# Pre-norm attention and expert layer: the second norm's rows are turned by VectorE through a DRAM scratch, and three small steps change engine or place

## The chip, the cores and the metric

The kernel runs on one core of a Trainium2 chip. A core has five engines with a queue of instructions each: TensorE (PE in the profile, its weight loads PEld), VectorE (DVE), ScalarE (ACT), GpSimd (POOL) and SyncE (SP), which only issues DMAs here. An engine takes its instructions in the order in which they are written; between engines there are semaphores. The metric is the device time of one execution in microseconds.

## The reference, cut to what matters

```python
x = hidden                                   # (2, 2048, 1024) f32, 4096 rows
h = layernorm(x)
q, k, v = h @ wq.T + bq, h @ wk.T + bk, h @ wv.T + bv      # 32 heads of 32 each
scores = einsum('bshd,bstd->bsht', q, k) / sqrt(32)   # over the HEADS of one row
context = einsum('bsht,bstd->bshd', softmax(scores), v)
x = x + context
h = layernorm(x)
gate = h @ gate_w.T                          # 8 experts, the best two are kept
w_full = one_hot(top2(gate)) * softmax(...)
low = h @ lora_A.T                           # 8 x 16 columns
x = x + h @ base_w.T + base_b + 2 * sum_e(w_full_e * low_e @ lora_B_e.T)
```

Attention runs between the 32 heads of one and the same row, so no row needs another one.

## The kernel before, in words

The 4096 rows are worked in T = 32 steps of P = 128 rows. Every f32 matmul operand is split into a float16 high part (a cast) and a float16 low part (original less high part), and a product is made of the terms high times high, high times low and low times high. The weights k, q, v, base and "ag" (lora_A with the gate, 136 columns) are split once, in the first two steps; where a weight's low part is all zero its term is skipped, which it is here for k, q and v, so a projection half of 512 columns is 16 matmuls (`project`, L1284).

Each engine's program is `pipeline` (L375): `step(0)`, `step(1)`, a loop over steps 2 to 30, `step(31)`, and a tail. A step t holds the attention front of tile t and the back of tile t-1 (called p = t-1 in the helpers). TensorE's order in a step before: first half of k (L1536); `context(t-1)`, 96 small matmuls of probabilities with v (L1541); second half of k; first half of q; the small matmul that spreads row statistics; second half of q; `turn2(t-1)`, 8 transposes of the normalised rows of tile t-1 (L1555); both halves of v; `experts(t-1)`, 24 matmuls with ag (L1562); `attend(scored)`, 96 small matmuls for the scores (L1568); `dense_all(t-1)` (L1456): 39 matmuls with base, `turn_low` (one transpose of the gated low-rank activations), 9 more, and `dense_lora` (L1433), which waits for `lowt_ready` and closes the sum.

The heads are turned by VectorE between the products: k's rows (`turn_first`, L1093), q's (L1204), v's (L1216) and the probabilities' (L1246). After each, ScalarE casts the high part (L743, L754, L759, L781) and VectorE or GpSimd subtracts to the low part: k's on VectorE (`first_low`), q's and v's on GpSimd (`second_lo` L529, `v_low` L535), the probabilities' on VectorE (L1253). The turned parts of k go out by 8 DMAs (`spread_k`, L424) into `diag`, block by block, because `attend` multiplies with block-diagonal operands; the parts of v are put there by 16 copies (`spread_v`, L356; line L360 in the rows), 12 on ScalarE and 4 on VectorE. `context` waits for all 16 and for the probabilities' low part.

The second norm: `attention_end` (L1066) turns the context back, adds the residual and takes the statistics; `norm2` (L1083) writes the normalised rows to `xn`; TensorE turns them (`turn2`) into `attn_ps`; ScalarE casts the high part `x2_hi` (L649), VectorE subtracts the low part `x2_lo` (L1004); then come `experts` and `dense`. The first norm of the next tile goes another way: its input is loaded a second time by DMAs that already permute 32-row blocks (`load_quads`, L416, four DMAs of 128-byte pieces), so one VectorE transpose (`turn_quads`, L993) turns it, and ScalarE casts it (`x1_high`, L644).

The gate (`gate_top` L1019, `gate_exp` L682, `gate_rest` L1029) gives `low`, the low-rank activations times the gate's weights; `turn_low` turns it on TensorE, and ScalarE's `low_copy` (L687, instruction L690) brings it back to SBUF and raises `lowt_ready`, for which `dense_lora` waits.

`soft` is the buffer of the softmax: written at L1226, and read for the last time at L1246.

Of the kernel before, what the change touches and what calls it, by code (L numbers as in the profile page):

```python
# [27 lines left out]
P = 128  # L28
# [37 lines left out]
def block_kernel(nc, x, wT, agT, lora_b, biases, out):  # L66
    T = x.shape[0] // P
    with ExitStack() as ctx:
# [166 lines left out]
        w_loaded = {g: [sem(f"w_{g}_loaded{k}") for k in range(KC)] for g in GROUPS}  # L235
# [111 lines left out]

        block = ctx.enter_context(nc.Block())
# [3 lines left out]
        x1_last = soft  # L352

# [18 lines left out]
        def rows(ap, t):  # L372
            return ap[bass.ds(t * P, P), :]

# [11 lines left out]
        def _(sp):  # L386
# [108 lines left out]
        def _(pool):  # L495
# [66 lines left out]
            def step(t, prev, nxt):  # L562
# [7 lines left out]
                if prev:  # L570
                    second_lo(t)
# [9 lines left out]
        def _(act):  # L581
# [52 lines left out]
            def x1_high(t):  # L634
# [5 lines left out]
                else:  # L640

                    act.wait_ge(x1_turned_ready, t)
                    act.wait_ge(scored, t)
                    nc.scalar.copy(x_hi[:, :, :], x1_turned).then_inc(xhi_ready, 1)  # L644

            def x2_high(p):

                act.wait_ge(turned2, p + 1)
                nc.scalar.copy(x2_hi, rows_ps).then_inc(x2hi_ready, 1)  # L649
# [80 lines left out]
            def step(t, prev, nxt):  # L730
# [15 lines left out]
                x2_high(t - 1)  # L746
# [7 lines left out]
                nc.scalar.copy(dense_parts[:, :, 0, :], turned3).then_inc(b_hi_ready, 1)  # L754

# [26 lines left out]
                if nxt:  # L782
                    for c in C_ACT_LAST:
# [12 lines left out]
        def _(dve):  # L796
# [208 lines left out]

            selectors()
# [76 lines left out]
            def norm2(p, x1):  # L1083
# [4 lines left out]
                else:  # L1088

                    dve.wait_ge(turned2, p)  # L1090
# [86 lines left out]
            def step(t, prev, nxt):  # L1177
                if not prev:
                    return first_step()
                if prev:  # L1180
# [10 lines left out]
                    norm2(t - 1, x1)  # L1191
                    turn_first(t)
# [7 lines left out]
                x2_low(t - 1)  # L1200
# [6 lines left out]
                add_bias(t, 0, "v", 1, v_acc, v_biased)  # L1207
                if nxt:
                    turn_quads(t + 1)
# [8 lines left out]
                if prev:  # L1218
                    gate_top(t - 1)

                dve.wait_ge(scored, t + 1)
                scores = attn_ps[:, :].rearrange("p (t c) -> p t c", t=QD)
# [5 lines left out]
                if one:  # L1228
                    base_split(6, 7)
                if nxt:  # L1230
# [47 lines left out]
        def _(pe):  # L1278
# [5 lines left out]
            def project(g, n, bank, done):  # L1284
# [14 lines left out]
                for k in range(KC):  # L1299
                    mm = nc.tensor.matmul(dst, x_lo[:, k, :], w_hi[g][:, k, cols], start=False, stop=(k == KC - 1))  # L1300
# [6 lines left out]
            def gram(g, first, last):  # L1307

                n_last = GRAM_CHUNKS[g] - 1
                for k in range(first, last):  # L1310
# [6 lines left out]
                    else:  # L1317
                        pe.wait_ge(w_loaded[g][k], 16)
# [86 lines left out]
            def experts(p):  # L1405

                pe.wait_ge(x2hi_ready, p + 1)
                pe.wait_ge(x2lo_ready, p + 1)
# [3 lines left out]
                for k in range(KC):  # L1412
                    nc.tensor.matmul(dst, x2_hi[:, k, :], ag_hi[:, k, :], start=(k == 0), stop=False)  # L1413
                    nc.tensor.matmul(dst, x2_hi[:, k, :], ag_lo[:, k, :], start=False, stop=False)  # L1414
                    mm = nc.tensor.matmul(dst, x2_lo[:, k, :], ag_hi[:, k, :], start=False, stop=(k == KC - 1))  # L1415
                mm.then_inc(ag_acc, 1)

# [22 lines left out]

            def dense_halves(p):

                pe.wait_ge(base_free, 2 * p + 1)
                dense(0, 0, KC)
# [11 lines left out]
            def dense_all(p):  # L1456

                pe.wait_ge(base_free, 2 * p + 1)
                dense(0, 0, KC)
# [68 lines left out]
            def step(t, prev, nxt):  # L1528
# [7 lines left out]
                project(FIRST, 0, 0, a_acc)  # L1536
                one = isinstance(t, int) and t == 1
                if one:
                    spread_flag(1)
                else:  # L1540
                    context(t - 1)  # L1541
# [6 lines left out]
                pe.wait_ge(v_biased, 2 * t)  # L1548
                project(SECOND, 0, 2, b_acc)
                if nxt:  # L1550
                    spread_stats(t + 1)

                pe.wait_ge(a_biased, 2 * t + 1)
                project(SECOND, 1, 0, b_acc)
                turn2(t - 1)  # L1555
# [6 lines left out]
                experts(t - 1)  # L1562
# [5 lines left out]
                attend(scored)  # L1568

                if one:  # L1570
                    dense_first()
# [65 lines left out]
```

## Time and profile before

| what | us |
|---|---|
| median of 3 runs | 1314.05 (1313.95 to 1314.11) |
| the profiled execution: device time | 1315.04 |
| the profiled execution: span of the core | 1313.2 |
| TensorE busy | 1286.7 (98%) |
| VectorE busy | 1106.1 (84%) |
| ScalarE busy | 672.4 (51%) |
| GpSimd busy | 278.7 (21%) |

The profile is one execution, taken by the hardware profiler. Its time line counts from the core's first instruction. Busy time is not the same as need: a matmul's row says when it was in the array, and whether its engine waited is read from the gaps and from what ended them. The loop's steps repeat closely; the step taken here as the example begins at 592.61 us and ends at 631.06 us.

### The profile page before, as it was taken

To read this page: it belongs to the slowest core of one execution; us is meant where nothing else is said; L and a number is where in the kernel's file an instruction comes from. 1 tells how busy PE (TensorE), PEld (TensorE's weight loads), DVE (VectorE), ACT (ScalarE), POOL (GpSimd) and SP (SyncE) were. 2 spreads that over 40 slices of the span, in tenths; PEclk is the share of its full clock that TensorE was granted. 3 is DMA by queue.
4 is the path that set the end of the run, shared out by engine and by line. 5 is a ranking of instruction groups with operands and counts; after the bars stand their busy time and mean duration, and the time that the engine had idled before them with its cause. 6 is when DMAs were issued, how large, how long until landed. Compare 5 with 4: busy or idle time off the path is not lost.

```text
span 1313.2 us, 30329 instructions
## 1 busy us (share of the span) xinstructions
PE 1286.7 (98%) x12506; PEld 682.2 (52%) x12506; DVE 1106.1 (84%) x1576; ACT 672.4 (51%) x1029; POOL 278.7 (21%) x305
## 2 busy tenths in 40 slices
PE   6899999999999999999999999999999999999998
PEld 4554554555555455555555555555555555555554
DVE  5799888888988888888888888888888888888885
ACT  4865445555444555544555554455554445545431
POOL 0212211212221121222112122211222221222220
PEclk9899999999999999999999999999999999999999
DMA  9732332221233222233322223322212322221210
GB/s 361 265 82 65 82 80 64 64 64 60 67 80 80 62 66 58 55 78 80 80 58 70 55 57 80 80 71 65 72 50 62 80 80 64 68 74 49 48 50 33
DMA packets 162011, 103.72 MB, mean 79 GB/s; under 512 B 135616, under 2 KB 136640, under 8 KB 161984
## 3 DMA queue, kind: packets, MB, share of 16 engines
q1 hardware_dynamic: 161984, 103.36, 28.1%
q8 instruction: 17, 0.28, 0.1%
q14 instruction: 10, 0.08, 0.0%
HBM read 69.78 MB, written 16.78 MB: 66 GB/s over the span
## 4 chain that ended last, share of the span: by engine, by line
PE 88%; DVE 6%; DMA 2%; ACT 1%; issue 1%; SPq 0%; DVEq 0%; POOL 0%; ACTq 0%
PE acc L1291 24%; PE acc L1300 24%; PE dense_acc L1430 23%; PE attn_ps L1383 7%; PE dense_acc L1438 4%; PE attn_ps L1391 2%; DMA work<-wT_dram 2%; PE low_ps L1414 1%; PE low_ps L1413 1%; PE low_ps L1415 1%; PE dense_acc L1453 1%; DVE w_lo_k L864 1%; DVE base_parts L864 1%; DVE v_parts L864 0%; DVE work L967 0%
## 5 line engine op out<-in xcount | busy, mean ns | idle before, releaser
L1430 PE MATMUL dense_acc<-base_parts,x 128*128 128x512 f16 x1488 | 330.1, 379 | 0.0
L360 ACT COPY work<-work 32x512 f16<-32x512 f16 x380 | 233.5, 614 | 8.5
L1430 PEld LDWEIGHTS dense_acc<-base_parts,x 128*128 128x128 f16 x1488 | 143.2, 98 | 167.2 <-issue 0.5
L967 DVE SCALAR_TENSOR_TENSOR work<-acc,acc_to_a,biases_sb 128x512 f32<-128x512 f32 x192 | 143.6, 749 | 47.2 <-PE acc L1300 44.6
L1291 PE MATMUL acc<-w_hi_q,x_hi 128*128 128x512 f16 x496 | 118.7, 383 | 0.0
L532 POOL TENSOR_TENSOR work<-work 128x1024 f16<-128x1024 f32 x32 | 68.2, 2131 | 237.3 <-ACT work L754 233.3
L1291 PE MATMUL acc<-w_hi_k,x_hi 128*128 128x512 f16 x496 | 117.5, 380 | 0.0
L1300 PE MATMUL acc<-w_hi_q,x_lo 128*128 128x512 f16 x496 | 117.3, 379 | 0.0
L1300 PE MATMUL acc<-w_hi_k,x_lo 128*128 128x512 f16 x496 | 117.2, 379 | 0.0
L1291 PE MATMUL acc<-v_parts,x_hi 128*128 128x512 f16 x496 | 117.2, 379 | 0.0
L1300 PE MATMUL acc<-v_parts,x_lo 128*128 128x512 f16 x496 | 117.2, 379 | 0.0
L759 ACT CAST work<-work 128x1024 f16<-128x1024 f32 x31 | 32.4, 1045 | 148.3 <-DVE work L1216 148.3
L510 POOL TENSOR_TENSOR columns<-columns 128x1 f32<-128x1 f32 x31 | 6.5, 209 | 479.5 <-ACT x_turned L666 464.4
L672 ACT COPY quad_stats<-low_ps 128x8 f32<-128x8 f32 x31 | 5.1, 165 | 194.4 <-PE low_ps L1397 194.4
L1383 PE MATMUL attn_ps<-work 128*32 128x128 f16 x6144 | 98.7, 221 | 3.9 <-POOL work L532 2.9
L1383 PEld LDWEIGHTS attn_ps<-work 128*32 128x32 f16 x6144 | 87.5, 98 | 21.4 <-issue 17.0
L538 POOL TENSOR_TENSOR work<-work 128x1024 f16<-128x1024 f32 x32 | 68.1, 2129 | 124.8 <-ACT work L759 114.6
L544 POOL TENSOR_TENSOR work<-work,biases_sb 128x1024 f32<-128x1024 f32 x32 | 76.0, 2374 | 33.0 <-DVE work L928 33.0
L754 ACT CAST work<-work 128x1024 f16<-128x1024 f32 x31 | 32.4, 1045 | 98.4 <-DVE work L1204 98.4
L1070 DVE STREAM_TRANSPOSE work<-attn_ps 128x1024 f32<-128x1024 f32 x32 | 62.4, 1952 | 21.4 <-PE attn_ps L1383 21.4
L1291 PEld LDWEIGHTS acc<-w_hi_k,x_hi 128*128 128x128 f16 x496 | 46.0, 98 | 64.4 <-issue 17.4
L1300 PEld LDWEIGHTS acc<-w_hi_q,x_lo 128*128 128x128 f16 x496 | 48.6, 98 | 58.9 <-issue 0.7
(200 smaller groups left out, 2139.2 us busy)
## 6 DMA issues: line engine op xcount, KB each, us to landing
work<-x_dram SPq DMA_DIRECT2D x64, 512.0 KB, 3.5
work<-work SPq DMA_DIRECT2D x256, 64.0 KB, 2.0
work<-x_dram SPq DMA_DIRECT2D x124, 128.0 KB, 3.3
out_dram<-work SPq DMA_DIRECT2D x31, 512.0 KB, 2.9
work<-wT_dram SPq DMA_DIRECT2D x16, 512.0 KB, 9.5
v_parts<-wT_dram SPq DMA_DIRECT2D x8, 512.0 KB, 14.5
base_parts<-wT_dram SPq DMA_DIRECT2D x5, 512.0 KB, 10.3
biases_sb<-bias_dram SPq DMA_DIRECT2D x4, 512.0 KB, 10.9
```

Of the source, the lines that this page charges most:

```text
L360: copy(diag[c * QD:(c + 1) * QD, :, c, j::NQ, :], src).then_inc(vdiag_ready, 1)
L532: nc.gpsimd.tensor_tensor(dense_parts[:, :, 1, :], turned3, dense_parts[:, :, 0, :], ALU.subtract).then_inc(b_lo_ready, 1)
L538: nc.gpsimd.tensor_tensor(v_parts_t[:, :, 1, :], turned3, v_parts_t[:, :, 0, :], ALU.subtract).then_inc(v_lo_ready, 1)
L544: nc.gpsimd.tensor_tensor(x1, x1, bias["base"][:, :], ALU.add).then_inc(x1_biased, 1)
L754: nc.scalar.copy(dense_parts[:, :, 0, :], turned3).then_inc(b_hi_ready, 1)
L967: nc.vector.scalar_tensor_tensor(out=ev[:, s], in0=acc[bank][:, :], scalar=acc_to_a[:, i:i + 1], in1=bias[g][:, s], op0=ALU.mult, op1=ALU. ...
L1070: nc.vector.transpose(turned.rearrange("p (h d) -> p d h", h=HEADS), attn_ps[:, :].rearrange("p (t d) -> p d t", t=QD)).then_inc(ctx_turne ...
L1291: nc.tensor.matmul(dst, x_hi[:, k, :], w_hi[g][:, k, cols], start=(k == 0), stop=False)
L1300: mm = nc.tensor.matmul(dst, x_lo[:, k, :], w_hi[g][:, k, cols], start=False, stop=(k == KC - 1))
L1383: mm = nc.tensor.matmul(attn_ps[c * QD:(c + 1) * QD, i4 * P:(i4 + 1) * P], dense_parts[:, i, dense_part, :], diag[:, spread_part, :, i, :] ...
L1430: nc.tensor.matmul(dense_acc[n][:, :], rows_part[:, k, :], w_part[:, k, cols], start=(k == 0 and m == 0), stop=False)
L1438: nc.tensor.matmul(dense_acc[n][:, :], low[:, :], lora_up[:, n * HALF:(n + 1) * HALF], start=False, stop=True).then_inc(base_acc, 1)
```

## The change

It has these parts:

1. `turn2` leaves the steps (it stays in the tail, for the last tile). In its place VectorE turns `xn` into `soft` in blocks of 32 by 32 (`turn_x2`, between `norm2` and `turn_first`); four DMAs of 128-byte pieces put the blocks where they belong in a DRAM scratch `turn_dram` (`park_x2`), two issued by SyncE and two by ScalarE; a fifth, issued by ScalarE, brings the whole back to `soft` (`fetch_x2`); ScalarE casts the high part from there, and the low part is subtracted by GpSimd (`x2_low` moves from VectorE).
2. q's low part moves from GpSimd (`second_lo`) to VectorE (`second_low`).
3. On ScalarE, `x1_high(t+1)` moves from between the copies of v to ahead of v's cast, and `low_copy(t-1)` from between the copies of v to behind the probabilities' cast.
4. On VectorE, `gate_top` moves behind the score's maximum and subtraction, which now also wait for `x2lo_ready`, since they write `soft`.
5. On TensorE, `context` goes inside the first half of k, after 10 of its 16 matmuls; the statistics' matmul goes one projection earlier; `experts` goes behind `attend`, and is cut in a high part and a low part, the second of which stands after 8 matmuls of `dense`.
6. The semaphores of v's weight loads are shared with k's, to make room for three new ones.

```diff
+        def park_x2(queue, p, quads):
+            queue.wait_ge(x2_turned, p + 1)
+            for q in quads:
+                src = x2_flat[q * QD:(q + 1) * QD, :].rearrange("c (k b t) -> c k b t", k=KC, b=NQ)
+                queue.dma_start(parked[q], src).then_inc(x2_parked, 16)
...
                     sp.dma_start(res, rows(x, t)).then_inc(res_loaded, 16)
+                    park_x2(sp, t - 1, (0, 1))
...
+            def x2_low(p):
+                pool.wait_ge(x2hi_ready, p + 1)
+                nc.gpsimd.tensor_tensor(x2_lo, x2_f32, x2_hi, ALU.subtract).then_inc(x2lo_ready, 1)
...
                 if prev:
-                    second_lo(t)
+                    x2_low(t - 1)
                 v_low(t)
...
+            def fetch_x2(p):
+                act.wait_ge(x2_parked, 16 * NQ * (p + 1))
+                act.dma_start(x2_flat, turn_dram).then_inc(x2_fetched, 16)
...
                     normalise_quads(t + 1)
+                park_x2(act, t - 1, (2, 3))
                 act.wait_ge(at_ready, t + 1)
...
                 nc.scalar.copy(k_parts[:, 0, :, :], turned3).then_inc(a_hi_ready, 1)
-                x2_high(t - 1)
+                fetch_x2(t - 1)
...
                 nc.scalar.copy(dense_parts[:, :, 0, :], turned3).then_inc(b_hi_ready, 1)
+                x2_high(t - 1)
+                if nxt:
+                    x1_high(t + 1)
...
-                for c in C_ACT_FIRST[:1]:
-                    spread_v(nc.scalar.copy, c)
-                if nxt:
-                    x1_high(t + 1)
-                    low_copy(t - 1)
-                for c in C_ACT_FIRST[1:]:
+                for c in C_ACT_FIRST:
                     spread_v(nc.scalar.copy, c)
                 act.wait_ge(pt_ready, t + 1)
                 nc.scalar.copy(dense_parts[:, :, 0, :], turned3).then_inc(p_hi_ready, 1)
                 if nxt:
+                    low_copy(t - 1)
                     for c in C_ACT_LAST:
...
+            def turn_x2(p):
+                dve.wait_ge(xn2_ready, p + 1)
+                dve.wait_ge(pt_ready, p + 1)
+                nc.vector.transpose(x2_flat, xn).then_inc(x2_turned, 1)
...
-            def project(g, n, bank, done):
+            def project(g, n, bank, done, inside=None):
...
                 for k in range(KC):
+                    if k == 2 and inside is not None:
+                        inside()
                     mm = nc.tensor.matmul(dst, x_lo[:, k, :], w_hi[g][:, k, cols], start=False, stop=(k == KC - 1))
...
+            def dense_half0(p):
+                pe.wait_ge(base_free, 2 * p + 1)
+                dense_terms(0, 0, 1, True)
+                experts_low(p)
+                dense_terms(0, 1, 3, False)
```

How it moves instructions, at three places. ScalarE in the loop's step, from the gate's exponential to the step's end; L360 (L371 after) is the copying of v's parts, `low<-low_ps` is `low_copy`. Before:

```order
L685 ACTIVATE columns<-columns 128x1 [waits gap_ready]
L766 ACTIVATE work<-work,columns 128x1024 [waits shifted]
L360 COPY work<-work 32x2x8x32 [waits scored,v_lo_ready]
L360 COPY work<-work 32x2x8x32 x3
L644 CAST x_hi<-x1_turned 128x1024 [waits scored,x1_turned_ready]
L690 COPY low<-low_ps 128x128 [waits low_turned]
L360 COPY work<-work 32x2x8x32 x4
L781 CAST work<-work 128x32x32 [waits pt_ready]
L360 COPY work<-work 32x2x8x32 x4
```

and in the changed kernel:

```order
L720 ACTIVATE columns<-columns 128x1 [waits gap_ready]
L805 ACTIVATE work<-work,columns 128x1024 [waits shifted]
L371 COPY work<-work 32x2x8x32 [waits scored,v_lo_ready]
L371 COPY work<-work 32x2x8x32 x7
L815 CAST work<-work 128x32x32 [waits pt_ready]
L725 COPY low<-low_ps 128x128 [waits low_turned]
L371 COPY work<-work 32x2x8x32 x4
```

`low_copy` has moved behind 8 copies and the cast that waits for the turned probabilities. VectorE in the loop's step, from the second norm to the turning of q; acc0 to acc2 are the projections' banks. Before:

```order
L928 TENSOR_SCALAR work<-work,mv,columns 128x1024 [waits rstd_ready2,turned2]
L1096 STREAM_TRANSPOSE work<-work 128x32x32 [waits a_biased]
L967 SCALAR_TENSOR_TENSOR work<-acc2,acc_to_a,biases_sb 128x512 [waits b_acc,at_ready]
L1101 TENSOR_TENSOR work<-work 128x1024 [waits a_hi_ready]
L967 SCALAR_TENSOR_TENSOR work<-acc0,acc_to_a,biases_sb 128x512 [waits b_acc]
L1004 TENSOR_TENSOR x2<-attn_ps,x2 128x1024 [waits x2hi_ready]
L1204 STREAM_TRANSPOSE work<-work 128x32x32 [waits a_lo_ready,b_biased]
L967 SCALAR_TENSOR_TENSOR work<-acc1,acc_to_a,biases_sb 128x512 [waits v_acc,bt_ready]
```

and in the changed kernel:

```order
L963 TENSOR_SCALAR work<-work,mv,columns 128x1024 [waits rstd_ready2,x2_turned]
L1045 STREAM_TRANSPOSE work<-work 128x1024 [waits pt_ready,xn2_ready]
L1143 STREAM_TRANSPOSE work<-work 128x32x32 [waits a_biased]
L1002 SCALAR_TENSOR_TENSOR work<-acc2,acc_to_a,biases_sb 128x512 [waits b_acc,at_ready]
L1148 TENSOR_TENSOR work<-work 128x1024 [waits a_hi_ready]
L1002 SCALAR_TENSOR_TENSOR work<-acc0,acc_to_a,biases_sb 128x512 [waits b_acc]
L1251 STREAM_TRANSPOSE work<-work 128x32x32 [waits a_lo_ready,b_biased]
L1002 SCALAR_TENSOR_TENSOR work<-acc1,acc_to_a,biases_sb 128x512 [waits v_acc,bt_ready]
L1050 TENSOR_TENSOR work<-work 128x32x32 [waits b_hi_ready]
```

The new transpose L1045 stands ahead of the turning of k; the subtraction L1004 is gone, and q's, L1050, has come in two rows below. TensorE at the start of the loop's step, k's first half and `context` (the low weights' eight are skipped by the branch). Before:

```order
L1291 MATMUL acc0<-w_hi_k,x_hi 128x512 x7
L1296 COMPARE_AND_BRANCH
L1298 MATMUL acc0<-w_lo_k,x_hi 128x512 x8
L1296 UNCONDITIONAL_BRANCH
L1300 MATMUL acc0<-w_hi_k,x_lo 128x512 x8
L1480 REGISTER_ALU
L1383 MATMUL attn_ps<-work 32x128 [waits p_lo_ready,vdiag_ready]
L1383 MATMUL attn_ps<-work 32x128 x95
```

and in the changed kernel:

```order
L1339 MATMUL acc0<-w_hi_k,x_hi 128x512 x7
L1344 COMPARE_AND_BRANCH
L1346 MATMUL acc0<-w_lo_k,x_hi 128x512 x8
L1344 UNCONDITIONAL_BRANCH
L1350 MATMUL acc0<-w_hi_k,x_lo 128x512 x2
L1545 REGISTER_ALU
L1433 MATMUL attn_ps<-work 32x128 [waits p_lo_ready,vdiag_ready]
L1433 MATMUL attn_ps<-work 32x128 x95
L1350 MATMUL acc0<-w_hi_k,x_lo 128x512 x6
```

Six matmuls of k's first half now follow `context`, and with them the end of that half.

## Rows read from the trace of the kernel before

**Rows 1.** The page, parts 1 and 4: busy time by engine, chain by engine.

```profile
PE 1286.7 (98%) x12506; PEld 682.2 (52%) x12506; DVE 1106.1 (84%) x1576; ACT 672.4 (51%) x1029; POOL 278.7 (21%) x305
...
PE 88%; DVE 6%; DMA 2%; ACT 1%; issue 1%; SPq 0%; DVEq 0%; POOL 0%; ACTq 0%
```

**Rows 2.** Busy time by stretch, steps 2 to 30 (us; PE, PEld, DVE, ACT, POOL; clock, DMA share, GB/s).

```profile
131.11:1246.39 1115.28, 1115.28 (x10876) 584.64 (x10877) 955.52 (x1338) 572.88 (x900) 246.94 (x261) 1.00 0.26 68
```

**Rows 3.** Time line of TensorE in one step: start us, us, engine, line, operation.

```profile
596.15 1.52 PE L1383 MATMUL attn_ps<-work 128*32 128x128 f16 x96
...
608.12 1.04 PE L1391 MATMUL attn_ps<-ident,work 128*128 128x128 f32 x8
608.99 1.89 PE L1291 MATMUL acc<-v_parts,x_hi 128*128 128x512 f16 x8
...
615.90 0.22 PE L1413 MATMUL low_ps<-ag_hi,x 128*128 128x136 f16 x1
...
617.41 1.52 PE L1383 MATMUL attn_ps<-work 128*32 128x128 f16 x96
...
629.35 1.88 PE L1438 MATMUL dense_acc<-lora_up,low 128*128 128x512 f32 x4
631.06 1.89 PE L1291 MATMUL acc<-w_hi_k,x_hi 128*128 128x512 f16 x8
```

**Rows 4.** Time line of VectorE, the same step; in brackets its idle time and releaser.

```profile
596.26 0.75 DVE L967 SCALAR_TENSOR_TENSOR work<-acc,acc_to_a,biases_sb 128x512 f32<-128x512 f32 x1 [0.64 <-PE acc L1300]
597.73 1.95 DVE L1070 STREAM_TRANSPOSE work<-attn_ps 128x1024 f32<-128x1024 f32 x1 [0.71 <-PE attn_ps L1383]
...
604.47 1.98 DVE L1096 STREAM_TRANSPOSE work<-work 128x1024 f32<-128x1024 f32 x1
...
616.88 2.17 DVE L1216 STREAM_TRANSPOSE work<-work 128x1024 f32<-128x1024 f32 x1
618.95 0.19 DVE L1021 TENSOR_SCALAR logits<-low_ps,w_undo_bits 128x8 f32<-128x8 f32 x1
...
619.54 1.21 DVE L1224 TENSOR_REDUCE top<-attn_ps 128x32 f32<-128x1024 f32 x1
620.79 1.23 DVE L1226 TENSOR_TENSOR work<-attn_ps,top 128x1024 f32<-128x1024 f32 x1
```

**Rows 5.** A group of VectorE by line, steps 2 to 30: busy us, mean ns, idle.

```profile
L993 DVE STREAM_TRANSPOSE x_turned<-work 128x1024 f32<-128x1024 f32 x29 | 35.8, 1234 | 0.0
```

**Rows 6.** Time line of ScalarE, the same step.

```profile
607.11 1.03 ACT L743 CAST work<-work 128x1024 f16<-128x1024 f32 x1
...
622.05 1.15 ACT L766 ACTIVATE work<-work,columns 128x1024 f32<-128x1024 f32 x1 [1.74 <-DVE work L1226]
623.11 2.52 ACT L360 COPY work<-work 32x512 f16<-32x512 f16 x4
...
627.60 0.27 ACT L690 COPY low<-low_ps 128x128 f32<-128x128 f32 x1 [0.90 <-PE low_ps L1421]
627.89 2.54 ACT L360 COPY work<-work 32x512 f16<-32x512 f16 x4
630.46 1.04 ACT L781 CAST work<-work 128x1024 f16<-128x1024 f32 x1
```

**Rows 7.** GpSimd and SyncE's DMA issues, the same step, by the time line.

```profile
598.31 2.96 SPq L422 DMA_DIRECT2D work<-x_dram  x4
...
608.17 4.99 SPq L428 DMA_DIRECT2D work<-work  x8
...
614.48 2.13 POOL L532 TENSOR_TENSOR work<-work 128x1024 f16<-128x1024 f32 x1 [7.47 <-ACT work L754]
```

**Rows 8.** The page, part 6: DMA issues, KB each, median us to landing.

```profile
work<-x_dram SPq DMA_DIRECT2D x64, 512.0 KB, 3.5
work<-work SPq DMA_DIRECT2D x256, 64.0 KB, 2.0
work<-x_dram SPq DMA_DIRECT2D x124, 128.0 KB, 3.3
```

More of the change, by code:

```diff
@@ L229, in block_kernel @@
         low_ps = ps("low_ps", [P, HALF])
-        w_loaded = {g: [sem(f"w_{g}_loaded{k}") for k in range(KC)] for g in GROUPS}
+        w_loaded = {g: [sem(f"w_{g}_loaded{k}") for k in range(KC)] for g in ("k", "q", "base")}
+        w_loaded["v"] = w_loaded["k"]
+        loads = {"k": 1, "q": 1, "v": 2, "base": 1}
         ag_loaded = sem("ag_loaded")
@@ L346, in block_kernel @@
         base_free = sem("base_free")
+        x2_turned = sem("x2_turned")
+        x2_parked = sem("x2_parked")
+        x2_fetched = sem("x2_fetched")
+        turn_dram = nc.dram_tensor("turn_dram", (P, HID), F32, kind="Internal").ap()
+        parked = turn_dram.rearrange("(b c) (k q t) -> q c k b t", b=NQ, k=KC, q=NQ)
         block = ctx.enter_context(nc.Block())
@@ L352, in block_kernel @@
         x1_last = soft
+        x2_flat = soft
+        x2_f32 = x2_flat.rearrange("p (k n) -> p k n", k=KC)
         C_ACT_FIRST, C_ACT_LAST, C_DVE = (0, 1), (2,), (3,)
@@ L642, in x1_high @@
                     act.wait_ge(x1_turned_ready, t)
-                    act.wait_ge(scored, t)
+                    act.wait_ge(v_acc, 2 * t)
                     nc.scalar.copy(x_hi[:, :, :], x1_turned).then_inc(xhi_ready, 1)
             def x2_high(p):
-                act.wait_ge(turned2, p + 1)
-                nc.scalar.copy(x2_hi, rows_ps).then_inc(x2hi_ready, 1)
+                if isinstance(p, int) and p == T - 1:
+                    act.wait_ge(turned2, 1)
+                    nc.scalar.copy(x2_hi, rows_ps).then_inc(x2hi_ready, 1)
+                else:
+                    act.wait_ge(x2_fetched, 16 * (p + 1))
+                    nc.scalar.copy(x2_hi, x2_f32).then_inc(x2hi_ready, 1)
+            def fetch_x2(p):
+                act.wait_ge(x2_parked, 16 * NQ * (p + 1))
+                act.dma_start(x2_flat, turn_dram).then_inc(x2_fetched, 16)
             x1_high(0)
@@ L1191, in step @@
                     norm2(t - 1, x1)
+                    turn_x2(t - 1)
                     turn_first(t)
@@ L1207, in step @@
                 add_bias(t, 0, "v", 1, v_acc, v_biased)
+                second_low(t)
                 if nxt:
@@ L1217, in step @@
                                     ev.rearrange("p (h d) -> p d h", h=HEADS)).then_inc(vt_ready, 1)
-                if prev:
-                    gate_top(t - 1)
                 dve.wait_ge(scored, t + 1)
+                dve.wait_ge(x2lo_ready, t)
                 scores = attn_ps[:, :].rearrange("p (t c) -> p t c", t=QD)
@@ L1229, in step @@
                     base_split(6, 7)
+                gate_top(t - 1)
                 if nxt:
@@ L1403, in turn2, with experts_high @@
                 turn_rows(turned2)
-            def experts(p):
+            def experts_high(p):
                 pe.wait_ge(x2hi_ready, p + 1)
-                pe.wait_ge(x2lo_ready, p + 1)
                 pe.wait_ge(lowt_ready, p + 1)
@@ L1414, in experts, with experts_low @@
                     nc.tensor.matmul(dst, x2_hi[:, k, :], ag_lo[:, k, :], start=False, stop=False)
-                    mm = nc.tensor.matmul(dst, x2_lo[:, k, :], ag_hi[:, k, :], start=False, stop=(k == KC - 1))
+            def experts_low(p):
+                pe.wait_ge(x2lo_ready, p + 1)
+                for k in range(KC):
+                    mm = nc.tensor.matmul(low_ps[:, 0:AG], x2_lo[:, k, :], ag_hi[:, k, :], start=False,
+                                          stop=(k == KC - 1))
                 mm.then_inc(ag_acc, 1)
+            def experts(p):
+                experts_high(p)
+                experts_low(p)
             def turn_low(p):
@@ L1535, in step @@
                 pe.wait_ge(b_biased, 2 * t)
-                project(FIRST, 0, 0, a_acc)
                 one = isinstance(t, int) and t == 1
                 if one:
+                    project(FIRST, 0, 0, a_acc)
                     spread_flag(1)
                 else:
-                    context(t - 1)
+                    project(FIRST, 0, 0, a_acc, lambda: context(t - 1))
                 pe.wait_ge(v_biased, 2 * t - 1)
@@ L1546, in step @@
                     context(0)
+                if nxt:
+                    spread_stats(t + 1)
                 pe.wait_ge(v_biased, 2 * t)
                 project(SECOND, 0, 2, b_acc)
-                if nxt:
-                    spread_stats(t + 1)
                 pe.wait_ge(a_biased, 2 * t + 1)
                 project(SECOND, 1, 0, b_acc)
-                turn2(t - 1)
                 pe.wait_ge(a_biased, 2 * t + 2)
@@ L1561, in step @@
                 project("v", 1, 2, v_acc)
-                experts(t - 1)
                 pe.wait_ge(ctx_turned, t)
@@ L1568, in step @@
                 attend(scored)
+                experts_high(t - 1)
                 if one:
+                    experts_low(0)
                     dense_first()
```

16 lines of the change are left out of this document (9 added, 7 removed).

## The prediction

> **What bounds the kernel now.** I read the busy shares and the chain that ended last first [rows 1]: TensorE is busy 98% of the span and is 88% of the chain; VectorE has 84%, and the reader should keep that second figure in mind. Then the stretch of steps 2 to 30 [rows 2]: 1115.28 us for 29 steps, 38.46 us each, TensorE busy in all of it, granted clock 1.00, which is the 2.4 GHz level. So 85% of the time is one step repeated, and the question is what a step costs afterwards. I use the step that ends at 631.06 [rows 3], so it began at 592.60, and lay each engine's queue anew with the durations of its rows, all times on that clock.
>
> **What TensorE gains.** `turn2` takes 608.12 to 608.99, 0.87 us [rows 3]; over the 30 steps that lose it 26 us. `experts` and the scores' matmuls only trade places (615.90 to 617.41 is 1.51 us of `experts`). Without waits TensorE would reach the scores at 617.41 - 0.87 - 1.51 = 615.03, and would need 629.35 - 617.41 + 1.51 = 13.45 from there to `dense_lora`, which takes 631.06 - 629.35 = 1.71 to the next step.
>
> **What VectorE's queue becomes.** Before, it takes k's first bias at 596.26, when that half ends, and the context's transpose at 597.73, when `context` ends [rows 4]: `context` is 1.47 long. Inside the half, `context` ends earlier, but the half ends 1.47 later, and the bias stands first in VectorE's queue: it starts at 597.73, the transpose at 598.48, 0.75 late. VectorE can't use the early context; it had idled 0.64 and 0.71 there and now idles in one piece. From the transpose to the turning of k is 6.74 (597.73 to 604.47), and now `turn_x2` comes in between. Its price is the nearest row, a transpose of the same form, 1.23 [rows 5]; not under that, not over the 2.17 of the slowest transpose [rows 4]. I take 1.28 with its wait. So k's turning starts at 606.50 and ends at 608.47. ScalarE's cast had started 0.66 after the transpose's end (604.47 + 1.98 = 606.45, then 607.11 [rows 6]), being late with other work; now it is free and casts 608.5 to 609.5. k's low part (1.23, as the subtraction of that size in [rows 4]) ends at 610.8, q's second bias (0.75) at 611.45. The `x2_low` that followed is gone. q is turned by 613.4 (1.94, as k's 1.98), its high part cast by 614.5, v's first bias hides behind that; q's low part, 2.13 on GpSimd [rows 7], is 1.23 here and ends at 615.8. Then `turn_quads` 1.23, bias, v's turning 2.17: until 619.8, against 619.05 before (616.88 + 2.17). `gate_top` no longer stands here (0.59, 618.95 to 619.54), so maximum and subtraction end at 622.25, against 622.02. VectorE has thus swallowed the new transpose nearly whole; what pays is the time in which it used to wait.
>
> **Two waits at the scores.** q's low part is there at 615.8. The k parts go out by 8 DMAs: issued from 608.17 in 4.99 [rows 7], the last 4.4 after the first, landing 2.0 later [rows 8]: 614.6 before; now from 609.55: 616.0. TensorE, ready at 615.03, waits until 616.0. That alone costs 0.97 and takes back the 0.87; by it TensorE would reach `dense_lora` at 629.45 and the next step at 631.16: **no change**.
>
> **The small copy decides.** `dense_lora` waits for `low_copy`. Before, it ran at 627.60 to 627.87 [rows 6], 1.5 ahead of need (629.35). In the changed queue it stands last: `gate_top` starts on VectorE behind the subtraction at 622.2 and takes about 0.65 (from 618.95 to just past 619.54 [rows 4]); the gate's exponential (0.2) follows on ScalarE, then the softmax's. That one began at 622.05 and the copies at 623.11, so copies now begin at 622.9 + 0.2 + 1.06 = 624.15. Eight copies are 2.54 + 2.57 (623.11 + 2.54; 627.89 to 630.46), so the cast of the probabilities starts at 629.25. It needs them turned: before, 4.1 after the gate's rest, now at about 628.8, so it doesn't wait for that. The cast takes 1.05, the copy 0.27: `lowt_ready` at 630.6. `dense_lora` starts 1.15 after TensorE is ready for it and 1.25 after its place before. With a little for the released weight load the next step begins at 632.35: **39.75 per step, 1.3 more than 38.46**. The wait can't be made up later: the next step's half of k starts VectorE's chain again, which ends in the same copy. `x1_high` ahead of v's cast is free (ScalarE idles there until v is turned).
>
> **The trip through DRAM.** No row shows a store of 128-byte pieces. The nearest is `load_quads`, 4096 such pieces in 4 DMAs of one queue: issued in 2.96 [rows 7], each landing 3.3 after its issue [rows 8], so 2.2 + 3.3 = 5.5 for all. With two queues the issues halve (1.5), the data doesn't: bounds 2.0 + 0.7 (a landing as the SBUF copies') and 5.5 + 3.3; I take 5.3. `turn_x2` ends at 606.55: all parked at 611.9, the fetch like a load of 512 KB, 3.5 [rows 8], up to 4.5: landed at 615.4 to 616.4. ScalarE is held at the fetch until 611.9 but has nothing due before q's cast at 613.4, a cover of 1.5. High part until 616.5, GpSimd's low part 2.13 until 618.7; `experts` wants the first at 617.5, VectorE the second at 619.8 because it must write `soft`. All fits, with 1.1 to spare, or 0.1 with the slow fetch. Beyond that each microsecond is one per step, 30 in all.
>
> The Trainium skill, "DMA: Bandwidth & Descriptors" (section Specifications), says that transfers under 512 B are done by read-modify-write, which speaks against exactly these stores. It gives no price; if it doubled the data's time the trip would be over its margin. No row of this kernel shows such a store.
>
> **The sum.** 29 steps by 1.3 are 37.7. Step 1 also has splits of base's weights in both queues; with one cast and one subtraction more of 1.1 to 1.3 in the path to the copy I take 4 (between 1.3 and 6). Step 31 and the tail keep the copy's old place; they lose `turn2` (0.87) and gain waits of the same size: +0.4. Together +42: on the profiled execution, 1315.04 (span 1313.2), 1357; the median of the runs is 1.0 lower than that execution, so **1356**.
>
> **Rivals.**
> 1. *The trip is late.* If stores of small pieces take twice the time (6.6 instead of 3.3 to landing), parked is 615.2, q's cast 1.8 late, x2's low part at 622 instead of 618.7, 2.2 after VectorE wants it: 2.2 more per step, 66 in all, 1422. Half as late: about 1385. This is also where the skill's rule would lead. For it: the path has six stations and 0.1 to 1.1 of slack. Against: the DMAs' mean share is 0.26 [rows 2]. Chance 0.24.
> 2. *The copy is hidden and only the scores wait.* It decides if `lowt_ready` comes by 629.45, 1.15 earlier than I have it (`gate_top` done earlier, or copies faster). Then -0.87 + 0.97 per step: 1314 to 1319. Chance 0.06.
> 3. *Faster:* TensorE waits at neither place, because DMAs of k land by 615.0 and the copy is done by 628.5. Then 30 steps by 0.87 less: 1314 - 26 = 1288. For it: 98% busy is what one reads first. Against: two queues are each over 1 late by their own durations. Chance 0.08.
> 4. That the change doesn't do what it says isn't likely: the queues above are read from its own order.
>
> **How the numbers follow.** The forecast has 0.62, with 1340 to 1376 as its own range (1.0 to 1.6 per step, step 1 at 1.3 to 6). The range reaches up into the late trip, 1340 to 1402, and leaves out rivals 2 and 3 (0.14) and the far part of rival 1 (0.06). Faster by over 0.2% has 0.08, within 0.2% (what a measurement of this kernel can tell from no change, 2.6 us) 0.05, slower 0.87.
>
> **What would show it.** Right: ahead of `dense_lora` TensorE idles about 1.2 with `low_copy` as releaser, in 29 steps; ahead of the scores it idles about 1 with the k DMAs or q's low part as releaser; VectorE idles 2 to 3 ahead of k's first bias; a step takes 39.7. ScalarE's `low_copy` starts within 0.1 of the probabilities' cast. The trip right: all parked 5.3 after `turn_x2`, and VectorE doesn't wait for `x2lo_ready`. Wrong: no idle time ahead of `dense_lora` (rivals 2, 3), or VectorE's maximum waiting for GpSimd (rival 1).

## The result, and the profile after

| | before | changed |
|---|---|---|
| median, us | 1314.08 (4 runs) | 1354.36 (1351.39 to 1355.89, 4 runs) |
| span of the profiled execution | 1313.2 | 1351.9 |
| a step, mean of steps 2 to 30 | 38.46 | 39.61 |
| start of step 2 | 131.11 | 135.97 |
| from the start of step 31 to the end | 66.8 | 67.3 |

The ratio is 1.0303, with a 95% interval of 1.0287 to 1.0318: 40 us slower. Of the 38.7 us by which the span grew, 33.4 lie in the 29 steps of the loop, 4.9 ahead of them, 0.5 behind. Step 30 alone is 41.93 long in this execution; the other 28 take 39.53 on average, and the time lines below are of one of these.

The page of the changed kernel, its lines that answer to [rows 1] and [rows 8]: busy times, the chain that ended last by engine, DMA issues with KB and median us to landing.

```profile
PE 1269.1 (94%) x12258; PEld 649.5 (48%) x12258; DVE 1138.9 (84%) x1607; ACT 673.2 (50%) x1029; POOL 278.7 (21%) x305
...
DVE 35%; PE 31%; ACT 12%; issue 12%; SPq 4%; DMA 4%; DVEq 2%; ACTq 0%; POOL 0%
...
work<-work SPq DMA_DIRECT2D x256, 64.0 KB, 2.7
work<-x_dram SPq DMA_DIRECT2D x124, 128.0 KB, 3.2
work<-turn_dram ACTq DMA_DIRECT2D x31, 512.0 KB, 4.0
...
turn_dram<-work SPq DMA_DIRECT2D x62, 128.0 KB, 3.5
turn_dram<-work ACTq DMA_DIRECT2D x62, 128.0 KB, 3.6
```

TensorE's busy time fell by 17.6 us with 240 transposes less, and the kernel grew by 40: TensorE was 88% of the chain and is 31%, VectorE was 6% and is 35%, ScalarE 1% and 12%. VectorE's busy share is the same 84% as before, so nobody would see from the busy shares that it now holds the kernel up; the chain shows it.

One step of the changed kernel, from 649.72 to 689.27 (39.55 us). TensorE's time line, for [rows 3]:

```profile
649.72 1.89 PE L1339 MATMUL acc<-w_hi_k,x_hi 128*128 128x512 f16 x8
...
651.97 1.52 PE L1433 MATMUL attn_ps<-work 128*32 128x128 f16 x96
653.43 1.47 PE L1350 MATMUL acc<-w_hi_k,x_lo 128*128 128x512 f16 x6
...
670.41 1.89 PE L1350 MATMUL acc<-v_parts,x_lo 128*128 128x512 f16 x8
673.86 1.52 PE L1433 MATMUL attn_ps<-work 128*32 128x128 f16 x96 [1.55 <-DMA work<-work]
...
687.45 1.98 PE L1498 MATMUL dense_acc<-lora_up,low 128*128 128x512 f32 x4
689.27 1.89 PE L1339 MATMUL acc<-w_hi_k,x_hi 128*128 128x512 f16 x8
```

`context` runs at 651.97, inside k's first half; the scores wait 1.55 for the DMAs of k. `dense_lora` shows no idle time here, but it starts at 687.45, 0.05 after the end of ScalarE's copy (687.40), and takes 1.82 to the next step instead of 1.71. The same step on VectorE, for [rows 4], and on ScalarE, for [rows 6]:

```profile
654.94 0.75 DVE L1002 SCALAR_TENSOR_TENSOR work<-acc,acc_to_a,biases_sb 128x512 f32<-128x512 f32 x1 [3.68 <-PE acc L1350]
655.61 1.94 DVE L1117 STREAM_TRANSPOSE work<-attn_ps 128x1024 f32<-128x1024 f32 x1
...
662.45 1.25 DVE L1045 STREAM_TRANSPOSE work<-work 128x1024 f32<-128x1024 f32 x1
663.62 1.93 DVE L1143 STREAM_TRANSPOSE work<-work 128x1024 f32<-128x1024 f32 x1
...
676.83 1.18 DVE L1271 TENSOR_REDUCE top<-attn_ps 128x32 f32<-128x1024 f32 x1
678.04 1.23 DVE L1273 TENSOR_TENSOR work<-attn_ps,top 128x1024 f32<-128x1024 f32 x1
```

```profile
668.73 0.34 ACTq L684 DMA_DIRECT2D work<-turn_dram  x1
...
672.74 1.04 ACT L679 CAST x<-work 128x1024 f16<-128x1024 f32 x1 [1.04 <-DMA work<-turn_dram]
...
679.93 0.20 ACT L720 ACTIVATE columns<-columns 128x1 f32<-128x1 f32 x1 [1.85 <-DVE columns L1074]
...
681.07 5.08 ACT L371 COPY work<-work 32x512 f16<-32x512 f16 x8
686.18 1.04 ACT L815 CAST work<-work 128x1024 f16<-128x1024 f32 x1
687.14 0.26 ACT L725 COPY low<-low_ps 128x128 f32<-128x128 f32 x1
```

Read as one chain: VectorE idles 3.68 ahead of k's first bias, although the context, which the next item in its queue reads, had ended by 653.5; its queue runs on to the subtraction (until 679.27), the gate's exponential on ScalarE waits for `gate_top`, the softmax's exponential and the eight copies stand behind that, then the cast, and only then the small copy.

### The profile page after: what moved, and what is told of

The parts are those of the page before. It is cut to its first block, busy times and chain, and to the rows that moved or that the text cites. A ratio compares the mean times of both kernels' runs of the same rounds, so it can differ in the third digit from the quotient of the medians.

```text
span 1351.9 us, 30110 instructions
## 1 busy us (share of the span) xinstructions
PE 1269.1 (94%) x12258; PEld 649.5 (48%) x12258; DVE 1138.9 (84%) x1607; ACT 673.2 (50%) x1029; POOL 278.7 (21%) x305
## 4 chain that ended last, share of the span: by engine, by line
DVE 35%; PE 31%; ACT 12%; issue 12%; SPq 4%; DMA 4%; DVEq 2%; ACTq 0%; POOL 0%
ACT work L371 6%; PE dense_acc L1519 6%; PE attn_ps L1433 5%; DVE work L1117 5%; PE dense_acc L1490 5%; DVE work L1143 5%; PE dense_acc L1498 5%; PE acc L1350 4%; SPq L446 4%; PE acc L1339 4%; DVE work L1002 4%; DVE work L1125 3%; DVE work L1251 3%; DMA work<-work 3%; ACT work L779 2%
## 5 line engine op out<-in xcount | busy, mean ns | idle before, releaser
L371 ACT COPY work<-work 32x512 f16<-32x512 f16 x380 | 233.5, 615 | 8.5
L1519 PE MATMUL dense_acc<-base_parts,x 128*128 128x512 f16 x768 | 176.5, 380 | 0.2 <-ACT x L675 0.2
L1490 PE MATMUL dense_acc<-base_parts,x 128*128 128x512 f16 x768 | 174.2, 379 | 0.0
L551 POOL TENSOR_TENSOR x<-work,x 128x1024 f16<-128x1024 f32 x31 | 67.1, 2165 | 281.4 <-ACT x L679 281.4
L1350 PE MATMUL acc<-w_hi_k,x_lo 128*128 128x512 f16 x496 | 122.4, 380 | 0.0
L1490 PEld LDWEIGHTS dense_acc<-base_parts,x 128*128 128x128 f16 x768 | 75.1, 98 | 85.9
L1519 PEld LDWEIGHTS dense_acc<-base_parts,x 128*128 128x128 f16 x768 | 73.0, 98 | 77.1 <-issue 0.8
L562 POOL TENSOR_TENSOR work<-work 128x1024 f16<-128x1024 f32 x32 | 68.1, 2130 | 75.2 <-ACT work L798 65.1
```

What stands on the lines that cost most here:

```text
L371: copy(diag[c * QD:(c + 1) * QD, :, c, j::NQ, :], src).then_inc(vdiag_ready, 1)
L562: nc.gpsimd.tensor_tensor(v_parts_t[:, :, 1, :], turned3, v_parts_t[:, :, 0, :], ALU.subtract).then_inc(v_lo_ready, 1)
L1490: nc.tensor.matmul(dense_acc[n][:, :], rows_part[:, k, :], w_part[:, k, cols], start=(k == 0 and m == 0), stop=False)
L1519: nc.tensor.matmul(dense_acc[n][:, :], rows_part[:, k, :], w_part[:, k, cols], start=(start and k == 0 and m == 0), stop=False)
```

## The experiments

Each was timed beside the kernel before on one chip; the table has the medians, and the step from the starts of `dense_lora` in steps 2 and 30 of each profile.

| run | us | before beside it | step, us |
|---|---|---|---|
| before, small copy late | 1356.1 | 1314.8 | 39.79 |
| changed, copy one place earlier | 1342.7 | 1314.8 | 39.22 |
| changed, no trip | 1348.4 | 1314.8 | 39.48 |
| changed, no trip, copy earlier | 1321.3 | 1314.8 | 38.54 |
| changed, `context` behind | 1330.1 | 1314.2 | 38.80 |
| changed, context's end first | 1308.5 | 1314.2 | 38.10 |
| the same, copy earlier | 1296.5 | 1314.2 | 37.77 |
| before, `context` inside | 1337.7 | 1315.4 | 39.26 |
| changed, one queue for the stores | 1355.0 | 1315.4 | 39.51 |
| changed, q's low part on GpSimd | 1348.3 | 1315.4 | 39.42 |

A limit below is one of the things for which TensorE can have to wait in a step; the one that ends last sets the step's length.

### The small copy alone, in the kernel before

```diff
                 if nxt:
                     x1_high(t + 1)
-                    low_copy(t - 1)
...
                 nc.scalar.copy(dense_parts[:, :, 0, :], turned3).then_inc(p_hi_ready, 1)
                 if nxt:
+                    low_copy(t - 1)
                     for c in C_ACT_LAST:
```

> The kernel before with one line moved: low_copy stands behind the cast of the probabilities, as in the change; everything else is as before. Theory (the small copy decides): the cast starts at about 629.3 on the example step's clock, the copy ends at 630.6, dense_lora starts 1.25 late, so 29 steps by 1.2 to 1.3: 1349 to 1353. Rival (VectorE's and ScalarE's queues have room, the copy is absorbed, and the change's loss comes from its waits at the scores): within 5 us of 1314.

Measured 1356.1, 1.0318 times the kernel before (1.0301 to 1.0336): 41 us, 1.33 per step. The time lines of ScalarE and TensorE at the end of a step:

```profile
648.55 0.26 ACT L690 COPY low<-low_ps 128x128 f32<-128x128 f32 x1
...
648.87 1.98 PE L1438 MATMUL dense_acc<-lora_up,low 128*128 128x512 f32 x4 [1.07 <-ACT low L690]
```

TensorE idles 1.07 for a copy of 0.26. This one line, a quarter of a microsecond of work on an engine that is half idle, costs as much as the whole change. The theory's mechanism is shown; its total was 3 short of the measured one, since a `dense_lora` that has waited takes 1.82 to the next step (648.87 to 650.69) and not 1.71, and step 1 pays too (step 2 starts at 133.43 instead of 131.11).

### The copy one place earlier, in the changed kernel

```diff
                 for c in C_ACT_FIRST:
                     spread_v(nc.scalar.copy, c)
+                if nxt:
+                    low_copy(t - 1)
                 act.wait_ge(pt_ready, t + 1)
                 nc.scalar.copy(dense_parts[:, :, 0, :], turned3).then_inc(p_hi_ready, 1)
                 if nxt:
-                    low_copy(t - 1)
```

> The changed kernel, low_copy one place earlier: behind the eight copies of v, ahead of the wait for the turned probabilities. It can then end about 1 us earlier (686.5 instead of 687.4 on the clock of the changed kernel's step that starts at 649.72). Theory (two limits of almost the same height: the copy frees dense_lora at 687.4, while the scores, which wait for the DMAs of k until 673.86, let TensorE come there at 687.3): 0.1 to 0.2 per step, 1348 to 1352. Rival (the copy alone makes the loss): the whole 1 us per step, about 1325.

Measured 1342.7: 11.6 less than the change, more than the 2 to 6 expected, far from the 29 of the rival. The step is 39.22, 0.4 shorter. From the scores to `dense_lora` it is 13.35 instead of 13.59 in the two steps shown, and `dense_lora` takes 1.72 to the next step instead of 1.82, which the expectation had left out; the long step 30 of the changed kernel (2.4 over the others) makes 0.08 of the mean. The limit that takes over, by TensorE's time line:

```profile
668.04 1.52 PE L1434 MATMUL attn_ps<-work 128*32 128x128 f16 x96 [1.54 <-DMA work<-work]
...
681.39 1.88 PE L1499 MATMUL dense_acc<-lora_up,low 128*128 128x512 f32 x4
```

The scores still wait 1.54, and from there to `dense_lora` it is 13.35 of uninterrupted work.

### Without the trip through DRAM, with the copy in both places

```diff
         def park_x2(queue, p, quads):
-            queue.wait_ge(x2_turned, p + 1)
...
-                queue.dma_start(parked[q], src).then_inc(x2_parked, 16)
+            pass
...
-                act.wait_ge(x2_parked, 16 * NQ * (p + 1))
-                act.dma_start(x2_flat, turn_dram).then_inc(x2_fetched, 16)
+                pass
...
-                    act.wait_ge(x2_fetched, 16 * (p + 1))
+                    act.wait_ge(x2_turned, p + 1)
```

> The changed kernel without the four stores and the fetch (the second norm's rows are used as VectorE's blocks leave them, so the product with them is of misplaced rows). Theory: the DMAs of k no longer share the DMA engines with the trip and land after 2.0 instead of up to 4.0, so the wait ahead of the scores falls from 1.6 to about 0.9; but the small copy holds dense_lora at the same place, so the time stays: 1348 to 1355, with the idle time moved from the scores to dense_lora. Rival (the trip is what costs): 0.7 per step or more, 1334 or less.

> Both of the last two edits: no trip through DRAM (misplaced rows), low_copy ahead of the wait for the probabilities. Theory: with both limits lowered the step falls by what neither gives alone, 0.7 to 0.8: 1328 to 1333. Rival (the two are independent and each gives its part): the sum of what the two runs beside it give.

Measured 1348.4 for the first, at the lower edge of what the theory allows: 6 less than the change. Of the 5.1 between the two profiled executions, 1.2 lie ahead of step 2 and 2.5 in step 30, where the changed kernel had its one long step; the other 28 steps are 0.04 shorter each. Its TensorE in one step:

```profile
671.54 1.52 PE L1429 MATMUL attn_ps<-work 128*32 128x128 f16 x96 [0.88 <-DMA work<-work]
...
685.77 1.98 PE L1494 MATMUL dense_acc<-lora_up,low 128*128 128x512 f32 x4 [0.71 <-ACT low L721]
```

The first DMA of k is issued 17.0 after the step's start in both kernels, and the scores start 7.1 after that issue with the trip and 6.5 without: only the landing changed. The wait ahead of the scores fell from 1.55 to 0.88, as forecast, and 0.71 of idle time came up ahead of `dense_lora`, with the small copy as its releaser: the time moved and did not go. With both edits the kernel takes 1321.3, below the range expected (1328 to 1333), and far from the sum of the two parts, about 1337: 33 us less than the change, where the two alone give 11.6 and 6. That is the mark of two limits of the same height: lowering one shows the other.

### `context` back behind the half

```diff
-                    project(FIRST, 0, 0, a_acc, lambda: context(t - 1))
+                    project(FIRST, 0, 0, a_acc)
+                    context(t - 1)
```

> The changed kernel with context put back behind the whole first half of k. Theory: VectorE's queue starts with k's first bias, which then has its operand 1.47 earlier; the transpose behind it has its own at the same time as before the change, so the whole chain comes 0.73 earlier and the step is 0.7 shorter: 1354 - 21 = 1333. Rival (context inside the half is what the early copies are for; it saves TensorE a wait, so putting it back costs): 1354 or more.

Measured 1330.1, 24 less than the change (1.0115, 1.0098 to 1.0132 of the kernel before). TensorE, in a step that begins at 640.33:

```profile
663.72 1.52 PE L1433 MATMUL attn_ps<-work 128*32 128x128 f16 x96 [0.80 <-DMA work<-work]
...
677.30 1.98 PE L1498 MATMUL dense_acc<-lora_up,low 128*128 128x512 f32 x4
```

Both limits come earlier, as both hang on VectorE's queue, whose transpose of the context starts 5.1 after the step's start instead of 5.9: the scores start at 23.4 instead of 24.1, the copy ends at 36.9 instead of 37.7.

### `context` inside the half, in the kernel before

```diff
-            def project(g, n, bank, done):
+            def project(g, n, bank, done, inside=None):
...
+                    if k == 2 and inside is not None:
+                        inside()
...
-                project(FIRST, 0, 0, a_acc)
...
+                    project(FIRST, 0, 0, a_acc)
...
-                    context(t - 1)
+                    project(FIRST, 0, 0, a_acc, lambda: context(t - 1))
```

> The kernel before with one part of the change alone: context inside k's first half from step 2 on. Theory (laying the queues anew with the rows' durations): context is now due 2.17 after the step's start, at 633.23, but ScalarE's last copies of v end at 634.06, so TensorE waits 0.85 there in each step; VectorE's chain, 0.75 later at its start, loses that again in its wait of 0.84 for v's second half. 29 steps by 0.85 to 0.9: 1336 to 1342. Rival (moving matmuls on the engine that is always busy changes nothing): within 4 us of 1314.

Measured 1337.7 (1.0169, 1.0152 to 1.0186), inside the range. The time line of TensorE:

```profile
643.38 1.52 PE L1385 MATMUL attn_ps<-work 128*32 128x128 f16 x96 [0.73 <-ACT work L360]
```

TensorE waits for ScalarE's last copies of v, which end at 643.32, 3.0 after this step's start. So this part costs in both kernels, but for two reasons: here because its operands aren't ready in time, in the changed kernel, where these copies end 0.7 after the step's start (689.96 against 689.27), because VectorE's first item waits for the end of the half.

### The context's end ahead of k's bias on VectorE

```diff
-                    add_bias(t, 0, FIRST, 0, a_acc, a_biased)
                     if one:
+                        add_bias(t, 0, FIRST, 0, a_acc, a_biased)
                         publish_flag(1)
                     attention_end(t - 1, x1)
+                    if not one:
+                        add_bias(t, 0, FIRST, 0, a_acc, a_biased)
```

> The changed kernel with VectorE's first two items swapped from step 2 on: the context's transpose and the norm's statistics ahead of k's first bias. Theory: the chain starts when context ends (3.7 after the step's start) and not when the half of k ends (5.1): everything after comes 1.3 to 1.4 earlier, both the DMAs of k and the small copy, and the step falls to 38.1 to 38.3: 1354 - 29 x 1.35 = 1312 to 1318. Rival (another queue takes over, the trip through DRAM or q's and k's halves waiting for bank 0): less than half of that, 1335 or more.

> The swap and low_copy ahead of the wait for the probabilities. Theory: the step is then held by the scores alone, at 38.0 to 38.1, or by TensorE's own 37.6: 1305 to 1315, faster than both kernels. Rival: the trip through DRAM, which ends no earlier than 10 us after the transpose, becomes the limit for VectorE's maximum, and nothing is gained over the run with the swap alone.

Measured 1308.5 and 1296.5. Both are below their ranges (1312 to 1318, 1305 to 1315). The first is 46 less than the change from a swap of two items in one queue; it is 0.9957 (0.9943 to 0.9971) of the kernel before. The second is **0.9863 (0.9846 to 0.9879)** of it, 18 us faster. Its time lines, TensorE and VectorE:

```profile
622.73 1.89 PE L1342 MATMUL acc<-w_hi_k,x_hi 128*128 128x512 f16 x8
...
626.61 1.95 DVE L1118 STREAM_TRANSPOSE work<-attn_ps 128x1024 f32<-128x1024 f32 x1 [1.94 <-issue]
...
645.26 1.52 PE L1436 MATMUL attn_ps<-work 128*32 128x128 f16 x96
...
658.61 1.88 PE L1501 MATMUL dense_acc<-lora_up,low 128*128 128x512 f32 x4
660.33 1.89 PE L1342 MATMUL acc<-w_hi_k,x_hi 128*128 128x512 f16 x8
```

VectorE starts on the context 3.9 after the step's start instead of 5.9. Neither the scores nor `dense_lora` wait in this step, which takes 37.60: that is the 38.46 of the kernel before less the 0.87 of `turn2`. In 8 of the 29 steps the scores still wait, 2.8 in all. Two thirds of the gain that the third rival had priced (18 of 26 us) were there, behind two queues' order.

### The stores on one queue, and q's low part back on GpSimd

```diff
-                    park_x2(sp, t - 1, (0, 1))
+                    park_x2(sp, t - 1, (0, 1, 2, 3))
...
-                park_x2(act, t - 1, (2, 3))
```

> The changed kernel with all four stores to the scratch issued by SyncE. Theory: the four issues take 2.7 instead of 1.6, the last lands about 0.7 later, the second norm's low part ends at 676.7 instead of 676.0 on the example step's clock, and VectorE's maximum starts at 676.8: it still fits, 1350 to 1358. Rival (the trip is already at its limit, and two queues are what keeps it there): 0.5 to 1 per step more, 1369 or more.

Measured 1355.0 against 1354.4: no difference in the time, but one in the step. In a step that begins at 649.71, TensorE's scores start at 673.41 after a wait of 1.13, and `dense_lora` at 687.37 after one of 0.44 for the small copy, where the changed kernel has 1.55 and none. Over the 29 steps these waits are 36.2 and 10.4 us, against 45.2 and 1.5. One queue thus lowers the scores' limit, and the copy hides it, as in the run without the trip. The stores themselves: four issues in a row land 2.7 each after their issue, where two and two land after 3.5 and 3.6, and the fetch, which waits for all four, is issued at 668.50, no later than with two queues (668.73). The expectation that the last would land 0.7 later was wrong. One queue with the copy moved earlier was not tried.

```diff
                 if prev:
                     x2_low(t - 1)
...
+                second_lo(t)
...
-                second_low(t)
```

(`second_lo(t)` stands ahead of `x2_low(t - 1)` on GpSimd.)

> The changed kernel with q's low part back on GpSimd, ahead of the second norm's low part there. Theory: GpSimd subtracts from 671.7 to 673.9, when the scores start anyhow (they wait for k's DMAs until 673.86), and VectorE, freed of 1.23, comes to the turning of v 0.9 earlier; the small copy is then no limit and the step is held by the scores alone, as in the run with the copy one place earlier: 1341 to 1347. Rival (GpSimd's 2.1 instead of 1.2 holds the scores): 1356 or more.

Measured 1348.3, 6 less than the change, though 1 above the range. TensorE and GpSimd:

```profile
673.54 1.52 PE L1433 MATMUL attn_ps<-work 128*32 128x128 f16 x96 [1.74 <-POOL work L556]
```

```profile
671.26 2.13 POOL L556 TENSOR_TENSOR work<-work 128x1024 f16<-128x1024 f32 x1 [6.90 <-ACT work L791]
```

The copy no longer holds `dense_lora`, but the scores now wait for GpSimd's subtraction, in 22 of 29 steps by the releaser, a little longer (1.74) than they had for the DMAs. So moving q's low part to VectorE was no gain in this arrangement: it cost 6 us.

Not tried alone were the other moves of parts 3 to 6: `x1_high`, `gate_top`, the statistics' matmul, `experts` and the shared semaphores. Of these `gate_top` stands on the way to the small copy.

## Why the prediction was right, point by point

**The step.** Forecast 39.75, measured 39.61 on average and 39.55 in the step shown. The time was forecast at 1356 and is 1354.4. The new transpose was priced at 1.28 with its wait; it is busy 1.25 (662.45), and between `norm2` and the turning of k VectorE's queue grew by 1.29 (661.60 to 663.62, against 603.74 to 604.47). VectorE's maximum was laid 27.2 after the step's start and is at 676.83 - 649.72 = 27.1. The copies begin 0.2 and the small copy ends 0.3 earlier than laid (37.7 against 38.0), in part since the softmax's exponential starts 0.1 behind the gate's and not 0.2.

**The small copy decides: right in mechanism, too strong in words.** The one-line run in the kernel before shows that it costs the whole 1.3 there. In the changed kernel it is one of two limits. The prediction named its signs, and the main one did not come: TensorE was to idle 1.2 ahead of `dense_lora` in 29 steps, and it idles 1.5 us there in all 29 together, in 7 of them, at most 0.3. No idle time at that place was even named as a sign of rivals 2 and 3, and it is neither: with the scores starting 24.1 after the step's start instead of 23.4, and 13.35 from there instead of 13.45, TensorE would reach `dense_lora` at 37.5 instead of 36.85, and the copy lets it go at 37.7. The copy's due time was right, and with it the step; the split of the waits was not. Nor does the time alone tell the two limits apart: with the scores' limit alone the kernel takes 1342.7, which is inside 1340 to 1376 too. That the forecast's other limit had almost the same height is luck. VectorE's wait ahead of k's first bias was forecast at 2 to 3 and is 3.68; `low_copy` starts at 687.14, within 0.1 of the cast's end, as said.

**The term that was mis-sized is the wait at the scores**: forecast 0.97, measured 1.55 in the step shown and 45.2 us in 29 steps. The prediction took 2.0 to landing for the DMAs of k from [rows 8]. The spread in this step:

```profile
L446 SPq DMA_DIRECT2D work<-work x8: 564/592/606, 666.7 to 671.1; - x8
...
DMA to landing us min/median/max: 2.0/2.7/4.0
```

These DMAs are in flight beside the stores and the fetch; without the trip they land after 2.0 again (median) and the wait is 0.88. The prediction weighed the trip only for its own length, not for what it does to the DMAs beside it. It cost nothing here because the copy hid it, by 0.2 (673.86 + 13.35 = 687.21 against 687.45). But it is most of why rival 2 was misjudged: "the copy is hidden and only the scores wait" was priced at 1314 to 1319, and the run that makes it true took 1342.7. Of the rest, 3.0 lie ahead of step 2, for which rival 2 had no term.

**The trip itself.** Forecast parked 5.3 after the transpose: the fetch is issued at 668.73, 5.0 after 663.70. Forecast 3.5 to 4.5 for the fetch: 4.0. Forecast the low part 26.1 after the step's start: 26.3, by GpSimd's time line

```profile
673.86 2.17 POOL L551 TENSOR_TENSOR x<-work,x 128x1024 f16<-128x1024 f32 x1 [8.99 <-ACT x L679]
```

0.8 before VectorE's maximum (676.83). Rival 1 didn't come to pass, except in step 30 of the profiled execution:

```profile
1267.95 1.72 PE L1433 MATMUL attn_ps<-work 128*32 128x128 f16 x96 [2.67 <-DMA work<-work]
```

There one issue among k's eight DMAs took 1.56 instead of 0.59, the fetch landed 5.2 after its issue instead of 4.0, and VectorE's maximum waited 0.37 for GpSimd's low part, the sign that the prediction had named for rival 1; the step is 2.4 longer. Why these DMAs were slow there is open.

The prediction doubled the stores' time in rival 1: they land 3.5 and 3.6 after their issue, against 3.2 for the loads with pieces of the same 128 bytes, so they don't take twice the loads' time. The Trainium skill, "DMA: Bandwidth & Descriptors" (Specifications), says that transfers under 512 B are done by read-modify-write. It states no price for that, and no run here can show one, since the loads have pieces under 512 B as well. How far the trip can be stretched before it costs was not tried.

**Step 1 and the ends.** Forecast 4 for step 1 and 0.4 for the end; measured 4.9 and 0.5. The cause of the 4.9 is in part another than the one given. TensorE's `dense_lora` in step 1, and the busy times and granted clock around it (columns as in [rows 2], the stretch's length first):

```profile
132.46 3.68 PE L1498 MATMUL dense_acc<-lora_up,low 128*128 128x512 f32 x4 [2.38 <-ACT low L725]
...
127.00:135.00 8.00, 5.46 (x16) 2.40 (x17) 7.74 (x12) 7.28 (x13) 0.00 (x0) 0.84 0.19 68
```

It starts 3.3 later than before (129.13) and takes 3.68 instead of 1.95, which is 1.5 of the 4.9: TensorE had waited 2.73 and 2.38 shortly before, and from 132.46 to 135.97 the granted clock is 0.51, the 1.2 GHz level. Without the trip the slow stretch comes earlier: after a wait of 2.71 the granted clock is 0.66 from 127.60 to 131.00, the 12 matmuls ahead of `dense_lora` take 4.44 instead of 2.75, and `dense_lora` then takes 1.98. So both runs pay about the same for the clock. The prediction had no term for it.

**The faster rival** had 0.08 at 1288. The change as it stands did not reach it, but with VectorE's first two items swapped and the copy earlier the kernel took 1296.5. What the prediction said against it, that two queues are each over 1 late, was true of the order and not of the work in them.

## What to carry to other kernels

Taking work off the engine that is busy 98% of the time gives its time back only if every engine that feeds it keeps its due times: lay each queue anew, instruction by instruction, and compare each handover with its need. A tiny operation in a long in-order queue is as late as what stands ahead of it; moving 0.26 us of work behind four copies and a cast cost 41 us. When two limits stand at the same height, an edit that lowers one shows little; test them together before calling one of them harmless, and look in the time line for idle time that has moved from one place to the other.

## What the runs showed of the hardware that was not expected

SBUF-to-SBUF DMAs of 64 KB, each 2.0 us from issue to landing when alone (minimum, median and maximum of a step of the kernel before), took up to 4.0 us beside the 128-byte stores and a 512 KB fetch, at a mean DMA share of 0.37 over the step. And the four stores were not done sooner through two queues than through one: the fetch that waits for them was issued 19.0 after the step's start with two and 18.8 with one, while the DMAs of k landed after 2.7 with two and 2.4 with one (medians).
